# Expert tiles written out; the second projection reads resident weights through registers

## What is computed

```python
def _L0_ffn_ref(x, router_W, router_b, W1, b1, W2, b2):
    logits = jnp.einsum('bsd,de->bse', x.astype(jnp.float32), router_W) + router_b
    probs = jax.nn.softmax(logits, axis=-1)
    top1 = jnp.argmax(probs, axis=-1)
    mask = jax.nn.one_hot(top1, N_EXPERTS, dtype=x.dtype)
    gates = mask * probs.astype(x.dtype)
    h = jax.nn.relu(jnp.einsum('bsd,edf->besf', x, W1) + b1[:, None, :])
    y = jnp.einsum('besf,efd->besd', h, W2) + b2[:, None, :]
    return jnp.einsum('bse,besd->bsd', gates, y)

x = x + 0.5 * ffn(_layernorm(x))
x = x + attention(_layernorm(x))      # linear attention, then a quantised MLP
x = x + 0.5 * ffn(_layernorm(x))
```

## Time and profile before

| | before |
|---|---|
| runs | 291.05, 294.88, 298.21 us |
| profiled execution | 290.7 us |
| its span, first to last instruction | 288.9 us |
| mean granted TensorE clock | 0.898 |
| busy: PE, DVE, ACT, POOL | 222.1, 114.3, 115.5, 139.1 us |
| first expert stage, first gather to last landing | 27.2 to 101.8 us |
| second expert stage, first gather to last landing | 199.8 to 275.0 us |
| copies of expert weights | 46 of 578 KB |

### The profile page before, as it was taken

One profiled execution on the slowest core, in us unless ns is written; L12 is line 12 of the kernel. 1 busy time (PEld: TensorE's weight loads), 2 busy tenths in 40 slices (PEclk: granted clock), 3 DMA queues, 4 the chain that ended last, 5 costly groups with the idle time before them and its releaser, 6 DMA issues.

```text
span 288.9 us, 4483 instructions
## 1 busy us (share of the span) xinstructions
PE 222.1 (77%) x1464; PEld 178.4 (62%) x1464; DVE 114.3 (40%) x448; ACT 115.5 (40%) x311; POOL 139.1 (48%) x200
## 2 busy tenths in 40 slices
PE   6969559856989958589888998998729698589600
PEld 3834459856889714567754678753529698589500
DVE  3497101111112142956769788576102011122131
ACT  2600123424346305698869564420133234346300
POOL 4803746657555519952226332303746675555530
PEclk9979776999599999999999999997978969899955
DMA  6998996667563150000000001216955766562163
GB/s 177 306 349 238 364 358 237 242 239 291 200 203 119 40 150 1 2 0 0 2 0 0 3 1 36 56 55 245 344 203 205 256 251 228 197 250 90 41 182 109
DMA packets 30723, 45.32 MB, mean 157 GB/s; under 512 B 3728, under 2 KB 22192, under 8 KB 30704
## 3 DMA queue, kind: packets, MB, share of 16 engines
q1 hardware_dynamic: 25648, 38.01, 36.6%
q0 software_dynamic: 2944, 6.04, 7.3%
q10 hardware_dynamic: 2112, 1.05, 1.2%
HBM read 11.69 MB, written 6.16 MB: 62 GB/s over the span
## 4 chain that ended last, share of the span: by engine, by line
PE 42%; issue 18%; ACT 10%; DVE 8%; another core or an unknown queue 8%; POOL 7%; DMA 4%; DVEq 0%; SPq 0%; ACTq 0%; POOLq 0%
PE bank L721 13%; PE bank L709 11%; ACT hT L509 5%; PE bank L850 5%; PE bank L841 4%; DMA xnT<-y_scratch 2%; POOL rstd L405 2%; PE bank L644 2%; DMA y_scratch<-ysb,dstu 2%; DVE x L1034 1%; PE bank L658 1%; PE bank L822 1%; ACT h L577 1%; PE bank L669 1%
## 5 line engine op out<-in xcount | busy, mean ns | idle before, releaser
L448 POOL DMA_INDIRECT y_scratch<-ysb,dstu x46 | 45.1, 981 | 44.2 <-DVE ysb L1018 39.4
L509 ACT ACTIVATE hT<-bank,ewc_own 128x128 f32<-128x128 f32 x96 | 27.2, 371 | 73.8 <-issue 41.7
L442 POOL DMA_INDIRECT Xg<-xn_scratch,srcu x46 | 44.5, 967 | 20.7 <-issue 13.4
L644 PE MATMUL bank<-ones_bf 128*128 128x512 bf16 x139 | 37.5, 419 | 5.4 <-DMA xnT<-y_scratch 2.9
L721 PE MATMUL bank<-ewc_own,hT 128*128 128x128 f32 x192 | 30.1, 307 | 13.0 <-ACT hT L509 8.6
L721 PEld LDWEIGHTS bank<-ewc_own,hT 128*128 128x128 f32 x192 | 27.2, 218 | 14.1 <-ACT hT L509 9.0
L709 PE MATMUL bank<-xT,ewc_own 128*128 128x128 f32 x192 | 30.8, 313 | 3.3 <-DVE xT L1013 3.3
L509 ACT ACTIVATE hT<-bank,actT 128x128 f32<-128x128 f32 x72 | 20.5, 368 | 27.2 <-PE bank L709 14.1
L709 PEld LDWEIGHTS bank<-xT,ewc_own 128*128 128x128 f32 x192 | 28.4, 227 | 4.5 <-DVE xT L1013 4.5
L1018 DVE TENSOR_TENSOR ysb<-bank,ewc_own 128x128 f32 (+1 forms) x24 | 7.0, 291 | 58.6 <-PE bank L721 31.8
L644 PEld LDWEIGHTS bank<-ones_bf 128*128 128x128 bf16 x139 | 14.1, 109 | 22.4 <-issue 5.3
(11 more groups left out here) (146 smaller groups left out, 347.8 us busy)
## 6 DMA issues: line engine op xcount, KB each, us to landing
ewc_own<-ew SPq DMA_DIRECT2D x24, 578.0 KB
actT<-ew SPq DMA_DIRECT2D x18, 578.0 KB
qb<-ew SPq DMA_DIRECT2D x4, 578.0 KB
ew<-in_L_ffn_W_dram SPq DMA_DIRECT2D x1, 2048.0 KB, 11.3
ew<-in_L_ffn_W_dram SPq DMA_DIRECT2D x8, 256.0 KB, 7.2
xnT<-y_scratch SPq DMA_DIRECT2D x8, 256.0 KB, 3.7
x<-in_L_attn_x_dram SPq DMA_DIRECT2D x4, 256.0 KB, 3.7
xn_scratch<-xn ACTq DMA_DIRECT2D x4, 256.0 KB, 6.3
```

Source lines behind the costliest of these rows:

```text
L442: g.indirect_dma_start(out=Xg[:, k % UNROLL, :], out_offset=None, in_=xn_scr, in_offset=bass.IndirectOffsetOnAxis(ap=srcu[:, k:k + 1], axis=0)
L448: g.indirect_dma_start(out=y_scr, out_offset=bass.IndirectOffsetOnAxis(ap=dstu[:, k:k + 1], axis=0), in_=ysb[:, k, :], in_offset=None).the ...
L509: last = A(hT[:, t.slot, c * P:(c + 1) * P], bank[2 + t.parity][:, c * P:(c + 1) * P], ACT.Relu, bias=ewc[t.ahead][:, B1_AT + c:B1_AT + c ...
L644: mm(bank[2][:, :], ones_bf[:, :], bc(ones_bf[:, :].unsqueeze(1), [P, 4, P]), start=True, stop=True)
```

## The change

- The loops over the tiles are gone: PE, ACT, DVE and SP have all 23 tiles written out, with constants in waits and addresses.
- In `ew` the order of the columns is now first weights, first bias, second bias, second weights. A copy takes only the first three: 2,576 bytes a partition. All eight slots are private.
- PE reads the second weights from `ew` itself, at an address that comes from a register. The 23 registers are loaded at the end of the routing (`load_experts`), and the warm-up behind it is halved to seven matmuls.
- POOL makes `prefer`, `before` and `ltE` ahead of its first normaliser instead of behind the fourth, and the waits for constants ask for smaller counts.

```diff
-W1_AT, W2_AT, B1_AT, B2_AT, EW = 0, F, F + FC * D, F + FC * D + FC, F + FC * D + FC + D
+W1_AT, B1_AT, B2_AT, W2_AT, EW = 0, F, F + FC, F + FC + D, F + FC + D + FC * D
+CW = W2_AT
...
-        ewc_own = sb("ewc_own", [P, UNROLL - 4, EW])
+        ewc_own = sb("ewc_own", [P, UNROLL, CW])
...
-                    sp.dma_start(ewc[t.ahead], ew[:, bass.ds(e, 1), :].squeeze(1)).then_inc(ewc_in[t.ahead], 16)
+                    sp.dma_start(ewc[t.ahead], ew[:, bass.ds(e, 1), 0:CW].squeeze(1)).then_inc(ewc_in[t.ahead], 16)
...
-                for k in range(UNROLL):
+                for k in range(NT):
+                    t = Tile(k)
+                    e = expert(t)
                     if k == FIRST:
                         sp.wait_ge(src_ready, m + 1)
-                    load_weights(Tile(0, k), expert(Tile(0, k)))
-
-                def step(i, n):
-                    done, t = Tile(i, n), Tile(i, n + UNROLL)
-                    e = expert(t)
-                    sp.wait_ge(y_ready, m * NT + 1 + done.k)
+                    if k >= UNROLL:
+                        sp.wait_ge(y_ready, m * NT + 1 + k - UNROLL)
                     load_weights(t, e)
-                expert_tiles(sp, step, NT - UNROLL)
...
-                pe.wait_ge(const_ready, 11)
+                pe.wait_ge(const_ready, 4)
...
-            def experts(m):
-                def turn(i, n):
-                    t = Tile(i, n)
+            def load_experts(m):
+
+                pe.wait_ge(eid_ready, m + 1)
+                return [pe.value_load(eid[0:1, k:k + 1], min_val=0, max_val=NE - 1) for k in range(NT)]
+
+            def experts(m, e):
...
                     for c in range(FC):
                         last = mm(bank[4 + t.parity][:, 0:D], hT[:, t.slot, c * P:(c + 1) * P],
-                                  ewc[t.ahead][:, W2_AT + c * D:W2_AT + (c + 1) * D], start=c == 0, stop=c == FC - 1)
+                                  ew[:, bass.ds(e[k], 1), W2_AT + c * D:W2_AT + (c + 1) * D].squeeze(1), start=c == 0, stop=c == FC - 1)
...
             sources(0)
-            keep_warm(WARM_GATHER)
-            experts(0)
+            e = load_experts(0)
+            keep_warm(WARM_GATHER // 2)
+            experts(0, e)
...
                 if m == 0 and g == 0:
-                    dve.wait_ge(const_ready, 11)
+                    dve.wait_ge(const_ready, 3)
...
                 dve.wait_ge(rank_ps, m + 1)
+                if m == 0:
+                    dve.wait_ge(const_ready, 8)
...
-                    v.tensor_tensor(out=ysb[:, bass.ds(t.k, 1), :].squeeze(1), in0=bank[4 + t.parity][:, 0:D],
-                                    in1=ewc[t.ahead][:, B2_AT:EW], op=ALU.add).then_inc(y_ready, 1)
+                    v.tensor_tensor(out=ysb[:, t.k, :], in0=bank[4 + t.parity][:, 0:D],
+                                    in1=ewc[t.ahead][:, B2_AT:W2_AT], op=ALU.add).then_inc(y_ready, 1)
```

More of the change, by code:

```diff
@@ L156, in macaron_kernel @@
         gelu_bias = sb("gelu_bias", [P, 1])
-        act_flat, qb_flat = actT.rearrange("p s c n -> p (s c n)"), qb.rearrange("p c n -> p (c n)")
-        ewc = ([ewc_own[:, u, :] for u in range(UNROLL - 4)]
-               + [act_flat[:, u * EW:(u + 1) * EW] for u in range(3)] + [qb_flat[:, 0:EW]])
+        ewc = [ewc_own[:, u, :] for u in range(UNROLL)]
         bank = [ctx.enter_context(nc.psum_tensor(f"bank{i}", [P, 512], f32)) for i in range(8)]
@@ L260, in macaron_kernel, with __init__ @@
         class Tile:
-            def __init__(self, i, n):
-                self.k, self.parity, self.slot = i * UNROLL + n, n % 2, n % RING
-                self.ahead, self.round = n % UNROLL, i + n // UNROLL
-        def expert_tiles(eng, step, tiles=NT):
-            loops = min(LOOPS, tiles // UNROLL)
-            with eng.Fori(0, loops) as i:
-                for n in range(UNROLL):
-                    step(i, n)
-            for k in range(loops * UNROLL, tiles):
-                step(loops, k - loops * UNROLL)
-        def left(i, n):
-            return not isinstance(i, int) or i * UNROLL + n < NT
+            def __init__(self, k):
+                self.k, self.parity, self.slot = k, k % 2, k % RING
+                self.ahead, self.round = k % UNROLL, k // UNROLL
         def wait_xn(eng, m, g):
@@ L376, in _ @@
                             pattern=[[-1, P]], channel_multiplier=1).then_inc(const_ready, 1)
+            g.iota(prefer[:, :], [[-1, NE]], base=NE, channel_multiplier=0,
+                   allow_small_or_imprecise_dtypes=True).then_inc(const_ready, 1)
+            g.affine_select(out=before[:, :], in_=before[:, :], compare_op=ALU.is_gt, fill=0.0, base=0,
+                            pattern=[[1, P]], channel_multiplier=-1).then_inc(const_ready, 1)
+            g.affine_select(out=ltE[:, :, :], in_=ltE[:, :, :], compare_op=ALU.is_gt, fill=0.0, base=0,
+                            pattern=[[1, NE], [-1, NE]], channel_multiplier=0).then_inc(const_ready, 1)
             def normaliser(at):
@@ L711, in up, with down @@
                     last.then_inc(h_ps, 1)
-                def down(i, n):
-                    t = Tile(i, n)
+                def down(k):
+                    t = Tile(k)
                     pe.wait_ge(hT_ready, m * NT + 1 + t.k)
-                    if not left(i, n + 1):
+                    if k + 1 == NT:
                         pe.wait_ge(y_ready, m * NT + t.k - 1)
@@ L721, in down @@
                         last = mm(bank[4 + t.parity][:, 0:D], hT[:, t.slot, c * P:(c + 1) * P],
[L722 removed]
+                                  ew[:, bass.ds(e[k], 1), W2_AT + c * D:W2_AT + (c + 1) * D].squeeze(1), start=c == 0, stop=c == FC - 1)
                     last.then_inc(y_ps, 1)
[L725 to L735 removed]
+                turn(0)
+                turn(1)
+                up(0)
+                for k in range(NT):
+                    if k + 2 < NT:
+                        turn(k + 2)
+                    if k + 1 < NT:
+                        up(k + 1)
+                    down(k)
             turn_xn(0, 0)
```

59 lines of the change are left out of this document (22 added, 37 removed).

## The result

The changed kernel takes 308.8 us (median of four runs, 306.9 to 314.8), where the kernel before took 293.3 us in the same session (a fourth run took 291.66). The ratio is 1.053, with a 95% interval of 1.048 to 1.059: slower. The prediction was 294 us, in a range that ended at 308.

A forecast was written before the change was run, and what follows sets the result against it. The prediction took POOL's scatters and gathers as the bound, with late PE results adding slack. Loads +12.4 and smaller copies -12 gave +0.4, 291.1 us profiled, put at 294 on the runs' scale, range 280 to 308.

The forecast's parts named there:

- What bounds the kernel: Expert stages, first to last scatter: POOL's scatters and gathers set a floor of 46.0 us; stretches took 57.6 and 58.2.
- the slack: Time over POOL's floor in both expert stages, 11.6 + 12.2 = 23.8 us, laid to PE results arriving late.
- Smaller copies, -12: Expert stages: copies cut from 578 to 322 KB would recover half of the slack, 12 us, bounds 0 and 23.8.
- the first stop: First expert stage, 36.8 to 41.7 us: PE's result waits for ACT, ending 2.0 us after POOL's tenth gather.
- The loads, 0.70 us each: PE before the warm-up: 23 register loads take 16.1 us a stage, first scatters +5.1 and +7.3, in sum +12.4 us.
- the scale: 4.2 us added to the profiled time, since the median of the runs stood that far above the profiled execution.
- The warm-up: PE behind the loads: seven matmuls from rest take 3.17 us; halving from 14 gives nothing back.
- Loops written out, 0: Tile loops: four backward branches on PE of 0.15 us median, about 0.6 us in all, counted as zero.
- The register steps of the second projection, 0: PE, second projection: four sequencer steps of 0.050 us a tile, taken as hidden; up to 9.2 us if not.
- POOL's constants, -2.1: Start of routing: DVE's first pick and the first stage's source list move up by 2.1 us.
- The one on the slower side: Rival, chance 0.30: stops stay, loads are paid in full, +12.4 us remains; 303 profiled, 307 on the scale.
- The rule on the load: PE's register loads: a skill page's floor of about 600 ns makes 23 loads 13.8 us; a measured 0.268 is below it.

The follow-up runs named there:

- e12: The kernel before, unaltered, traced on a chip without late signals: 262.3 us, one run.
- e4: The changed kernel with copies of the biases alone (528 bytes a partition), first projection reading expert 0's weights: 308.0 us, one run.
- e5: The changed kernel with POOL's gathers replaced by plain DMAs of consecutive rows on SyncE: 273.8 us, one run.
- e6: The changed kernel with POOL's scatters replaced by plain DMAs of consecutive rows on SyncE: 272.9 us, one run.
- e1: The kernel before with its tile loops written out and nothing else: 290.7 us, 0.995 of the kernel before.
- e8: The kernel before with tile loops written out and POOL's constants made early, no register loads, full copies: 287.9 us, 0.982 of the kernel before.
- e16: The kernel of e8 with POOL also waiting for a newer PE signal before gathers, chip without late signals: 259.1 us, 0.988 of the kernel before.
- e18: The changed kernel with four loads ahead of the warm-up, the others among the tiles, chip without late signals: 259.4 us, 0.991 of the kernel before.
- e9: The kernel of e8 with five gathers ahead of the first scatter instead of ten: 283.8 us, 1.087 of the kernel before.
- e7: The kernel before plus the block of 23 register loads on PE in both stages, registers unread: 321.9 us, 1.104 of the kernel before.

## Why the prediction was wrong, point by point

**What bounds the kernel.** Right. POOL's floor of 46.0 us and the slack of 23.8 us over it, read from the earlier trace rows, are what e12 shows when the stops are absent: 45.9 and 46.0 us. The prediction laid the late results to gathers and copies in flight together; e4 takes the copies out of that.

**Smaller copies, -12.** This step failed, and 12 of the 17 us by which the sum (291.1 profiled) missed 308.2 are its. The prediction had bounds of 0 and 23.8, named for the lower one that the first stop ends with the last gather and not with the copies, and then took half, for which no row spoke. In the stretches the value is 0: the stretches became 57.4 and 59.9 us, 59.1 and 59.5 with the loads spread, 59.7 and 58.5 with copies of 66 KB. In its place the runs show that the late signals go when half of POOL's indirect DMAs go (e5, e6), stay with the DMA engines at 0.25 (e4), and are absent on other chips with these at 0.92 (e12). The high share in the stop of the earlier trace rows was a companion, not the cause.

**The loads, 0.70 us each.** The mechanism was right: program order on PE, paid ahead of the first transpose, partly hidden in the old stop. The size was low. The blocks took 17.7 and 17.2 us, 0.77 and 0.75 each instead of 0.70: most loads took 0.64 with their steps, not 0.56, and in the first block eight of the 23 loads alone took 0.54 to 0.77, in the second seven took 0.52 to 0.80. The first block ended at 41.0, not 39.5. From the first transpose to the first scatter it was 5.8 and 5.7 us, not 5.4. So the first scatters came 6.9 and 9.1 us later, not 5.1 and 7.3: 3.6 us of the miss.

**The additions.** The terms from the first transpose to the first result add up to 5.1 us; the prediction has 5.2 and then counts 5.4. And 291.1 with the 4.2 us of the scale is 295.3, not 294. Neither slip is over 1.3 us.

**The warm-up.** Seven matmuls took 3.16 us, as the earlier trace rows had it.

**Loops written out, 0.** Right within one half per cent (e1). The Trainium skill, in Runtime: NRT & Kernel Launch, section Instruction fetch mechanics, prefers code written out because a taken branch out of the resident pages forces a fetch. The trace has no such price: the branches on PE took 0.24 us at most before, e1 gained 0.0 to 0.9% without them, and its stops stood as before (stretches of 56.5 and 57.6 us).

**The register steps of the second projection, 0.** Right where PE sets the pace: with these steps in place it needs 1.89 us a tile in the window of e5, busy for 41.2 of 41.6 us.

**POOL's constants, -2.1.** Right: `key` stands at 12.20. That the block starts at 23.33, where 23.4 was said, is in part luck. The source matmuls ended at 23.5 (21.01 + 2.51), 2.6 us earlier than before and not 2.1, and the sequencer was 0.2 us ahead of them, not 0.6.

**The rest of the stretches.** The second grew by 1.7 us. The profiled executions with late signals spread from 56.4 to 59.9 us for like stretches, so I read nothing into it.

**The rivals.** The one on the slower side, stops that stay and loads paid in full, is what happened. It gave 303 profiled with loads of 0.70 us and named the point from which it decides. The range ended at 308 because it left out loads above 0.75 us without relief, and they took 0.77 and 0.75.

**The rule on the load.** The Trainium skill, in DMA: Bandwidth & Descriptors, section Latency and other measured facts, puts such a load at about 600 ns at least. The rows of e4 and of the change differ from it: in the change the load itself takes 294 ns at the least, in e4 0.30 us for nearly all, and it is 0.64 only with the two steps of its check. The measurement decides. The estimate from that page, 23 times 600 ns or 13.8 us, is lower than all blocks measured.

## What to carry to other kernels

Steps of a sequencer that stand ahead of the first work of a stage delay all of it, less only what the stage would have waited for anyway. In the change two blocks of 23 loads took some 35 us. Its first scatters came 16 us later in sum where a stop had stood before, and 23 us later where none had. With four loads ahead and the others among the tiles the kernel was as fast as before. When an engine reacts late, a busy neighbour at that moment is only a suspect: halve each suspect alone (bytes in e4, the number of indirect DMAs in e5 and e6) before a gain is counted. And where a cost lies between 0 and a large number and the only row that bears on it speaks for 0, take 0.

The best kernel found is that of e8, the change without its registers and smaller copies: 0.982 of the kernel before on a chip with late signals and 0.994 to 0.995 on two without. On the second of these e16 and e18 are not told from it.

## What the runs showed of the hardware

While POOL sends indirect DMAs 0.30 us apart, PE's signals can reach ACT and DVE late, and not on every chip. In the first session and on the two chips of e1 to e8, save in e5 and e6, signals came 1 to 6 us late several times in each expert stage. On the three chips of e9 to e18 ACT took not one tile more than 0.04 us late, in e12 with all 46 indirect DMAs of a stage in one row without a break. The kernel before takes 290 to 298 us on the one kind and 260 to 263 on the other. What sets the two kinds apart isn't known. Of e1 to e18 no chip was met in two sessions, and all with late signals were measured before all without, so that something that changed in time fits as well as the chip. It also stays open whether POOL's indirect DMAs are the cause or only the condition, and whether shorter rows help where signals are late, since the runs meant for that met the other kind.

A register load of the PE sequencer from SBUF takes 0.30 us (e4, copies of 66 KB), and single ones up to 0.80 us beside copies of 322 KB (the change) and 1.05 beside 578 KB (e7). The medians of the 46 loads are 0.301, 0.306 and 0.447 us.
